# Layer-1 experts that write their results straight to the output, in a two-layer graph network on one core

## The reference

```
# x: (3125, 256), after layer 1's two attentions were added to it
xf = layernorm(x)                                  # the normed rows
idx = argmax(xf @ router_w.T + router_b, axis=-1)  # one of 32 experts per row
h   = relu(xf @ W1[idx] + b1[idx])                 # 256 -> 64
y   = relu(h @ W2[idx] + b2[idx])                  # 64 -> 256
out = x + y                                        # x is the row before the norm
```

## Time and profile before

| | kernel before |
|---|---|
| median of three runs | 3251.31 us |
| the profiled execution, its own time | 3242.09 us |
| its span (first to last instruction) | 3240.5 us |
| instructions | 49670 |
| PE / DVE / POOL / ACT busy, of the span | 69% / 64% / 53% / 38% |
| mean granted TensorE clock | 0.795 of full speed |

### The profile page before, as it was taken

The page is one execution under the profiler, slowest core; times in us unless marked ns, Lnnn a source line. Parts: engine busy times, 40 slices in busy tenths (PEclk is TensorE's granted clock), DMA queues, the critical chain, the costliest instruction groups (busy, mean ns, idle before and its releaser), DMA issues. The chain is left out here.

```text
span 3240.5 us, 49670 instructions
## 1 busy us (share of the span) xinstructions
PE 2249.1 (69%) x10992; PEld 1511.7 (47%) x10993; DVE 2061.8 (64%) x3849; ACT 1246.3 (38%) x3616; POOL 1712.3 (53%) x1802
## 2 busy tenths in 40 slices
PE   3635887867997389948674799997662666654693
PEld 2322333345555356525563678776552444433341
DVE  7587777778888343352576788887593656665221
ACT  3223333326775212233101567765201667652010
POOL 1586777733554301132554877774466777751213
PEclk9866777678999599979776899998755989885555
DMA  4768888875785278835996788886896555530444
GB/s 140 206 181 234 262 260 261 264 231 144 218 217 157 101 252 284 265 94 185 370 395 207 236 270 281 278 280 167 248 312 175 150 147 147 148 103 23 132 152 132
DMA packets 456711, 673.21 MB, mean 208 GB/s; under 512 B 67154, under 2 KB 333836, under 8 KB 456001
## 3 DMA queue, kind: packets, MB, share of 16 engines
q1 hardware_dynamic: 334017, 357.96, 35.9%
q0 software_dynamic: 87248, 263.43, 27.2%
q10 hardware_dynamic: 35296, 50.06, 4.3%
HBM read 494.85 MB, written 177.80 MB: 208 GB/s over the span
## 5 line engine op out<-in xcount | busy, mean ns | idle before, releaser
L1532 POOL DMA_INDIRECT xn<-table,src_col x572 | 591.1, 1033 | 180.0 <-issue 156.2
L1573 PE MATMUL sum_h_ps<-xn,sum_h_hot 128*128 128x261 f32 (+1 forms) x1936 | 530.6, 417 | 185.8 <-DVE xn L1587 142.7
L1573 PEld LDWEIGHTS sum_h_ps<-xn,sum_h_hot 128*128 128x128 f32 x1936 | 371.7, 202 | 336.8 <-DVE xn L1587 241.7
L1092 POOL DMA_INDIRECT arena_a<-table,src_col x264 | 265.2, 1005 | 270.2 <-issue 184.6
L978 POOL DMA_INDIRECT arena_b<-table,src_col x336 | 318.5, 948 | 111.7 <-issue 109.6
L1587 DVE TENSOR_TENSOR xn<-xn,al 128x514 f32<-128x514 f32 (+1 forms) x352 | 243.5, 692 | 161.8 <-DMA xn<-table,src_col 158.5
L1596 DVE TENSOR_TENSOR arena_a<-arena_a,sum_h_ps 128x522 f32 (+1 forms) x440 | 246.1, 559 | 64.8 <-issue 41.1
L1706 PE MATMUL sum_ps<-xn,sum_hot 128*128 128x264 f32 x880 | 245.8, 407 | 31.1 <-DVE arena_a L1729 10.9
L999 PE MATMUL score_ps_hd<-arena_a,score_hot 128*128 x1320 | 254.7, 346 | 0.0
L1689 POOL TENSOR_TENSOR xn<-xn,al 128x264 f32<-128x264 f32 x220 | 154.9, 706 | 171.8 <-DMA xn<-edge_h 169.8
L1009 ACT ACTIVATE xn<-score_ps_en 128x512 f32<-128x512 f32 x220 | 131.5, 598 | 293.3 <-PE score_ps_en L995 289.1
(11 more groups left out here) (516 smaller groups left out, 4632.9 us busy)
## 6 DMA issues: line engine op xcount, KB each, us to landing
xn<-edge_h SPq DMA_DIRECT2D x220, 264.0 KB, 3.1
edge_h<-arena_b SPq DMA_DIRECT2D x84, 528.0 KB, 4.6
arena_b<-kept SPq DMA_DIRECT2D x66, 516.0 KB, 5.3
xn_t<-edge_rows SPq DMA_DIRECT2D x110, 256.0 KB, 4.6
score_h_hot<-hots SPq DMA_DIRECT2D x220, 128.0 KB, 13.4
kept<-arena_a ACTq DMA_DIRECT2D x40, 516.0 KB
xn<-kept SPq DMA_DIRECT2D x66, 257.0 KB
arena_a<-in_f_w SPq DMA_DIRECT2D x16, 1024.0 KB, 8.5
```

The source lines that it names most:

```text
L1092: pool.indirect_dma_start(rows[:, q, s, :], None, table, bass.IndirectOffsetOnAxis(ap=K.src_col[:, w * SUB + s:w * SUB + s + 1], axis=0)). ...
L1532: pool.indirect_dma_start(rows[w][:, s, 0:RW], None, table, bass.IndirectOffsetOnAxis(ap=K.src_col[:, w * SUB + s:w * SUB + s + 1], axis=0 ...
L1573: ins = pe.matmul(ps[:, u, b, 0:part], lhsT=hot[:, w % QH, s, :], rhs=rows[w][:, s, b * part:(b + 1) * part], start=(s == 0), stop=(s == S ...
```

## The change

- `slots1` rows become 513 words (2052 bytes) wide: the normed row, the row before the norm (the token sum `x`), and the node's number as an integer. `finish_route_l1` builds these rows in `arena_a`: DVE's second addition writes to `total_x` there and not to `K.x`, ACT's norm writes beside it, and POOL writes the numbers with one `iota`. Since `arena_a` also holds what the additions read, the chunks go from the last tiles to the first (`tile_of`).
- The earlier blanking writes zeros and the number 3125 in each row, in 28 DMAs for the 14 of before, each of about the same size.
- In `experts_l1` the load brings 2052-byte rows. DVE's `result` first copies the numbers to a small tile, then computes relu(PSUM) + x in one instruction (`scalar_tensor_tensor`). POOL scatters the result by the numbers into the output; rows with number 3125 are out of bounds and left out. Since `result` now reads the rows' buffer, the next load into it waits for the result (`s_yb`) and not for `down` (`s_y`). The weights' load keeps its wait on `s_y`.
- `combine_l1` is gone, and with it the array `y_slots1`.

```diff
@@ segment_softmax
-        blanks = K.slots1.shape[0] // (4 * P) if H == H0 else 0
-        zeros = K.arena_b[:, 5 * 1024:6 * 1024]
+        blanks = K.slots1.shape[0] // (2 * P) if H == H0 else 0
+        zeros = K.arena_b[:, 5 * 1024:5 * 1024 + 2 * SLOT1]
...
-                    sp.dma_start(K.slots1[r * 4 * P:(r + 1) * 4 * P, :].rearrange("(p j) d -> p (j d)", j=4), zeros[:, :]).then_inc(s_blank, 16)
+                    sp.dma_start(K.slots1[r * 2 * P:(r + 1) * 2 * P, :].rearrange("(p j) d -> p (j d)", j=2), zeros[:, :]).then_inc(s_blank, 16)
...
-                pool.memset(zeros[:, :], 0.0).then_inc(s_zeros, 1)
+                pool.memset(zeros[:, :], 0.0).then_inc(s_wiped, 1)
+                pool.wait_ge(s_wiped, 1)
+                pool.iota(zeros.rearrange("p (j d) -> p j d", j=2)[:, :, 2 * D].bitcast(I32), [[0, 2]], base=NOBODY, channel_multiplier=0).then_inc(s_zeros, 1)
@@ finish_route_l1
+        both = K.arena_a[:, :].rearrange("p (t r) -> p t r", t=NT)
+        xn, total_x, token = both[:, :, 0:D], both[:, :, D:2 * D], both[:, :, 2 * D].bitcast(I32)
+        def tile_of(n):
+            return NT - U - n // U * U + n % U
...
+            pool.wait_ge(s_gone, 1)
+            pool.iota(token, [[P, NT]], base=FIRST_TOKEN, channel_multiplier=1).then_inc(s_token, 1)
+            pool.wait_ge(s_token, 1)
             pool.wait_ge(s_slot, 1)
             for t in range(NT):
-                pool.indirect_dma_start(K.slots1, bass.IndirectOffsetOnAxis(ap=K.slot_to[:, t:t + 1], axis=0), K.xn[:, t, :], None).then_inc(s_sent, 16)
+                pool.indirect_dma_start(K.slots1, bass.IndirectOffsetOnAxis(ap=K.slot_to[:, t:t + 1], axis=0), both[:, t, 0:SLOT1], None).then_inc(s_sent, 16)
...
+                if c == chunks - 1:
+                    dve.sem_inc(s_gone, 1)
...
-                    ins = dve.scalar_tensor_tensor(K.x[:, t, :], K.tab2[:, t, 0:D], f2[:, t, 0:1], K.x[:, t, :], ALU.mult, ALU.add)
+                    ins = dve.scalar_tensor_tensor(total_x[:, t, :], K.tab2[:, t, 0:D], f2[:, t, 0:1], K.x[:, t, :], ALU.mult, ALU.add)
@@ experts_l1
-        sizes = {"rows": D, "w": 2 * F1 + D, "xs_t": 2 * P, "h_t": P, "y": D}
+        sizes = {"rows": SLOT1, "w": 2 * F1 + D, "xs_t": 2 * P, "h_t": P, "y": D}
+        token = st.sbuf("token", [P, Q], I32)
...
-                pe.wait_ge(s_yb, j + 1)
+                pe.wait_ge(s_yb, j + 1 + Q - U2)
...
-                act.wait_ge(s_y, j + 1)
+                act.wait_ge(s_yb, j + 1)
                 act.dma_start(rows[:, q, :], K.slots1[bass.ds(j * P, P), :]).then_inc(s_in[q], 16)
...
-                dve.tensor_scalar(y[:, q, :], ps_y[:, q % U2, 0:D], 0.0, None, ALU.max).then_inc(s_yb, 1)
+                dve.tensor_copy(token[:, q:q + 1], rows[:, q, 2 * D:SLOT1].bitcast(I32))
+                dve.scalar_tensor_tensor(y[:, q, :], ps_y[:, q % U2, 0:D], 0.0, rows[:, q, D:2 * D], ALU.max, ALU.add).then_inc(s_yb, 1)
...
-            dve.sem_inc(s_yb, U2)
+            dve.sem_inc(s_yb, Q)
...
-                    pool.wait_ge(s_yb, j + 1 + U2)
+                    pool.wait_ge(s_yb, j + 1 + Q)
                     pool.nop(nofuse=True)
-                    pool.dma_start(K.y_slots1[bass.ds(j * P, P), :], y[:, q, :]).then_inc(s_out[q], 16)
+                    pool.indirect_dma_start(out, bass.IndirectOffsetOnAxis(ap=token[:, q:q + 1], axis=0), y[:, q, :], None,
+                                            bounds_check=N - 1, oob_is_err=False).then_inc(s_out[q], 16)
@@ combine_l1: removed whole
```

More of the change, by code:

```diff
@@ L165, in norm_tiles, with chunk_moments @@
     return T
-def chunk_moments(dve, step, K, T, c, s_var):
+def chunk_moments(dve, step, x, T, c, s_var):
     part = slice(c * U, (c + 1) * U)
@@ L423, in _ @@
             for c in range(NT // U):
-                chunk_moments(dve, step, K, T, c, s_var)
+                chunk_moments(dve, step, lambda t: K.x[:, t, :], T, c, s_var)
             for c in range(NT // U):
@@ L2566, in _ @@
             pe.wait_ge(s_w, 32)
-            for t in range(NT):
-                pe.wait_ge(s_xn, t + 1)
-                if t >= 2:
-                    pe.wait_ge(s_xt, t - 1)
-                pe.transpose(ps_x[:, t % 2, 0:P], K.xn[:, t, 0:P], K.ident[:, :])
-                pe.transpose(ps_x[:, t % 2, P:D], K.xn[:, t, P:D], K.ident[:, :]).then_inc(s_turn, 1)
-                if t >= 1:
-                    logits_of(t - 1)
+            for n in range(NT):
+                t = tile_of(n)
+                pe.wait_ge(s_xn, n + 1)
+                if n >= 2:
+                    pe.wait_ge(s_xt, n - 1)
+                pe.transpose(ps_x[:, n % 2, 0:P], xn[:, t, 0:P], K.ident[:, :])
+                pe.transpose(ps_x[:, n % 2, P:D], xn[:, t, P:D], K.ident[:, :]).then_inc(s_turn, 1)
+                if n >= 1:
+                    logits_of(n - 1)
             logits_of(NT - 1).then_inc(s_logits, 1)
@@ L2589, in _ @@
             for c in range(chunks):
-                chunk_norm(act, K, T, c, s_var, s_std, s_rstd, s_xn)
-                for t in range(c * U, (c + 1) * U):
-                    act.wait_ge(s_turn, t + 1)
-                    act.activation(K.xn_t[:, :, t * P:(t + 1) * P], ps_x[:, t % 2, 0:D].rearrange("p (k n) -> p k n", k=2), ACT.Copy).then_inc(s_xt, 1)
+                part = slice(c * U, (c + 1) * U)
+                act.wait_ge(s_var, c + 1)
+                act.activation(T["std"][:, part], T["var"][:, part], ACT.Sqrt, bias=K.eps[:, 0:1]).then_inc(s_std, 1)
+                act.wait_ge(s_rstd, c + 1)
+                for n in range(c * U, (c + 1) * U):
+                    act.activation(xn[:, tile_of(n), :], total_x[:, tile_of(n), :], ACT.Identity, scale=T["rstd"][:, n:n + 1], bias=T["shift"][:, n:n + 1]).then_inc(s_xn, 1)
+                for n in range(c * U, (c + 1) * U):
+                    t = tile_of(n)
+                    act.wait_ge(s_turn, n + 1)
+                    act.activation(K.xn_t[:, :, t * P:(t + 1) * P], ps_x[:, n % 2, 0:D].rearrange("p (k n) -> p k n", k=2), ACT.Copy).then_inc(s_xt, 1)
         @block.vector
@@ L2794, in _ @@
                     j = i * Q + q
-                    pool.wait_ge(s_yb, j + 1 + U2)
+                    pool.wait_ge(s_yb, j + 1 + Q)
                     pool.nop(nofuse=True)
-                    pool.dma_start(K.y_slots1[bass.ds(j * P, P), :], y[:, q, :]).then_inc(s_out[q], 16)
+                    pool.indirect_dma_start(out, bass.IndirectOffsetOnAxis(ap=token[:, q:q + 1], axis=0), y[:, q, :], None,
+                                            bounds_check=N - 1, oob_is_err=False).then_inc(s_out[q], 16)
             for q in range(Q):
                 pool.wait_ge(s_out[q], 16 * turns)
-def combine_l1(prog, K, out):
-    with Stage(prog, "join1") as st:
-        y = K.xn
-        s_y = [st.sem_sw(f"y{c}") for c in range(NT // U)]
-        s_sum, s_out = st.sem("sum"), st.sem("out")
-        block = st.block()
-        @block.gpsimd
-        def _(pool):
-            st.clear_stale(pool)
-            for t in range(NT):
-                pool.indirect_dma_start(y[:, t, :], None, K.y_slots1, bass.IndirectOffsetOnAxis(ap=K.slot_to[:, t:t + 1], axis=0)).then_inc(s_y[t // U], 16)
-        @block.vector
-        def _(dve):
-            for c in range(NT // U):
-                dve.wait_ge(s_y[c], 16 * U)
-                part = y[:, c * U:(c + 1) * U, :]
-                dve.tensor_tensor(part, part, K.x[:, c * U:(c + 1) * U, :], ALU.add).then_inc(s_sum, 1)
-        @block.sync
-        def _(sp):
-            for c in range(NT // U):
-                sp.wait_ge(s_sum, c + 1)
-                whole = U if c < NT // U - 1 else U - 1
-                sp.dma_start(out[c * U * P:(c * U + whole) * P, :].rearrange("(t p) d -> p t d", p=P), y[:, c * U:c * U + whole, :]).then_inc(s_out, 16)
-            sp.dma_start(out[(NT - 1) * P:N, :], y[0:NLAST, NT - 1, :]).then_inc(s_out, 16)
-            sp.wait_ge(s_out, 16 * (NT // U + 1))
 def stages(prog, K, A, out):
@@ L2853, in stages @@
     finish_route_l1(prog, K, A)
-    experts_l1(prog, K, A)
-    combine_l1(prog, K, out)
+    experts_l1(prog, K, A, out)
 class Keep:
```

24 lines of the change are left out of this document (13 added, 11 removed).

## The result

The changed kernel takes 3329.78 us (median of 4 runs, 3323.89 to 3331.93), the kernel before 3254.18 us on the same chip (4 runs, 3249.6 to 3258.67). The ratio is 1.0237, with a 95% interval of 1.0222 to 1.0252: slower by some 76 us, where 28 us less had been forecast. The profiled execution took 3331.93 us, its span is 3330.4 us.

What follows compares the result with a forecast made beforehand. A circle of waits through load latency, not PE, was taken to pace the experts' loop. Terms -43.0 + 14.3 + 0 + 0.3 + 0.4 = -28.0 us took 3251.3 to 3223.3 us; range 3210 to 3244, 8 times in 10.

Steps and rivals of the forecast that it cites:

- rival 3: Layer 0's blanking outgrows its stage: at 204 GB/s it ends some 18 us past it; 3241 us, chance 0.04.
- Blanking: Layer 0's zero writes: 14.7 MB for 7.3, taking 36 to 40 us, hidden behind DVE; cost 0.
- Only the last landing counts: Layer 1 routing: 25 scatters cost POOL what they did; only the last one lands later, +0.4 us (0 to +0.8).
- The sentence on the Trainium skill: Rows' load in the experts' loop: descriptors off 256-byte boundaries fetch unused bytes; under 2 us in all.
- The end of the program: Adding stage removed, last scatter and a 4.6 us DRAIN now at the end; -43.0 us.
- The order of the link: Experts' loop: load, PE's transposes, `down`, next load, 6.00 us; waiting for `result` makes the last part 1.95 for 1.40.
- The loop: Experts' loop: the load's wait for `result` adds 0.55 us a link over 26 links, +14.3 us.
- step (b): Experts' loop: rows' load of 257 KB for 128, taken as 0; bounds -4.2 to +12.0 us in all.
- rival 1: Experts' loop: the load's size counts in full, +0.46 us a link, +12.0 us; 3235.3 us, chance 0.22.
- Rival 2: Experts' loop: loads land as with busy DMA engines, 5.3 us for 3.0, +60; 3283 us, chance 0.06.
- rival 4: Experts' loop: scatters don't hide or another circle closes, +26 to +43 us; 3235 to 3252, chance 0.06.
- The start of the loop: Experts' loop: three loads of twice the size ahead of the first weights, +0.3 us (0 to +1).

Runs made afterwards that it cites:

- wait_result: Kernel before with one wait moved: the load waits for DVE's result, not for the second matmul; 3238.06 us for 3242.7, ratio 0.9983.
- p520: Changed kernel with slots1 rows 520 words (2080 bytes) long and apart; 3218.05 us for 3239.66 of the kernel before, ratio 0.9934.
- joined: Write-only stage added to a kernel with 2080-byte rows: 12 DMAs of 4104-byte pieces side by side; 42.7 us.
- odd: Same added stage: 12 DMAs of 2052-byte pieces, two a partition, side by side; 42.5 us.
- near_odd: Added write-only stage: 25 POOL scatters of 128 rows of 2052 bytes, each DMA's rows side by side; median landing 15.3 us.
- woven: Added write-only stage: 4104-byte pieces side by side, but neighbouring pieces given to successive DMAs; 36.5 us for 12 DMAs.
- even: Added write-only stage: 12 DMAs of 4096-byte pieces side by side; 16.9 us.
- quad: Added write-only stage: 12 DMAs of 4112-byte pieces side by side; 18.7 us.
- apart: Added write-only stage: 12 DMAs of 4104-byte pieces placed every 4160 bytes, with a gap; 17.0 us.
- both shifts: Added write-only stage: two groups of 12 DMAs, 4096-byte pieces every 4160 bytes, starting 8 or 4 bytes in; 17.0 and 17.7 us.
- far: Added write-only stage: 12 DMAs of 2052-byte pieces, two a partition, every 2112 bytes, starting 4 bytes in; 19.6 us.
- far_odd: Added write-only stage: 25 POOL scatters of 2052-byte rows, a row's neighbours in the DMAs before and after; landing 2.8 us.
- near_pair: Added write-only stage: 25 POOL scatters of 128 rows of 2056 bytes, each DMA's rows side by side; 3.7 us for 3.0.
- pair: Added write-only stage: 12 DMAs of 2056-byte pieces, two a partition, side by side; 22.3 us.
- the skips: Added write-only stage: two groups of 12 DMAs, 4104-byte pieces every 8208 bytes, starting at 0 or 4104; 23.1 and 22.3 us.
- probe_sent: Kernel with 2080-byte rows and eight loop buffers, plus a write-only stage of three SP groups and four POOL scatter groups; 3449.84 us, before 3244.68.

## Why the prediction was wrong

The time lies 86 us above the range's upper end of 3244. The sign was decided by writes that the prediction had set at 0.0 and 0.4 us. Its rival 3 names the first of the places, with a chance of 0.04 and a price of 18 us where 74 were lost.

**The steps that failed.**
- *"Blanking: ... 36 us, to 741, or 40 us at 370. Cost 0; the cover is gone below ... 272 GB/s."* The cover was sized well, the rate was not: 114 GB/s in place of 407 to 370, 129 us in place of 36 to 40, +74.2 us. The row taken as the nearest was that of 2064-byte rows, 16 bytes times 129; the new pieces were 4104 bytes side by side. Nearness was judged by size, and what decided, as far as the runs tell, was where the pieces meet. Rival 3 came close ("pieces of 4104 bytes at odd addresses": it is not the address alone, a start off by 8 bytes cost 0.1 us in 17) but halved the rate by choice, to 204 GB/s, without a row that bounds it. No row of before bounds it well. In one stretch rows of 1028 bytes, an odd number of words as here, are stored side by side, and the DMA engines stand at 0.79 and move 212 GB/s; the queues' rows of the same stretch (packets, MB, share) show whose time that is:

```profile
2440.00:2460.00 20.00, 2.45 (x12) 1.80 (x10) 1.58 (x4) 0.00 (x0) 15.13 (x17) 0.64 0.79 212
```
```profile
q0 software_dynamic: 767, 2.10, 48.3%
q10 hardware_dynamic: 2204, 2.13, 30.9%
```

The stores (q10) move 2.13 MB at a share of 0.309, that is 345 GB/s at a full share; it is the gathers of 1028-byte rows (q0) that stand at 217. They stand at 269 (a share of 0.378 for 6.11 MB) from 2560 to 2620, where no such store runs, so the stores may cost them something. It is a warning at most, not a rate.

- *"257 KB in 1.29 us is 204 GB/s, half of what the engines do. Only the last landing counts: +0.4 us."* True at 2080 bytes (206 GB/s at a share of 0.53, routing 112.4 us), wrong at 2052: the engines do 80 to 156 GB/s, a backlog forms behind an issue that looks unchanged, and +29.3 us stand at the stage's end. The test that I gave for it (more than 1.3 us a scatter on POOL) couldn't find this: POOL only issues. What tells is the landing and the distance from the last issue to the DRAIN.
- The sentence on the Trainium skill stands beside this. The Trainium skill, page "DMA: Bandwidth & Descriptors", section "How a descriptor splits into AXI transactions", was weighed as the rule against such rows. It speaks of reads, and no run here sets rows of this length on and off such a boundary for reading; for writes the trace gives it next to nothing: a start off by 8 bytes, with a gap, took 17.0 us for 16.9. Another page of the Trainium skill, "Collectives: The Full Stack", section "Rules for kernel authors", asks for 32-byte aligned buffers, to prevent a read-modify-write in the hardware; it speaks of collectives, and I had not weighed it. It points in the direction of the loss, but 32 bytes is not what these runs show: rows of 2064 bytes, whose every second boundary is off 32, lost nothing.

**The terms that held.** The end of the program: behind the last scatter's landing a DRAIN of 4.62 us (forecast 4.6), and 9.8 us from the start of tile 54's result to the end for the 9.5 rebuilt, so -42.7 us for -43.0. The order of the link, and 1.96 us from `down` to the next issue for the 1.95 worked out. The scatter in the loop hidden (970 ns, landing in 2.4 us, POOL waiting for DVE). POOL's cost of the routing scatters, 0.97 and 0.30 us.

**The terms that were mis-sized.** The loop: +14.3 forecast. From the load of tile 7 to that of tile 55 are 24 links and 154.2 us (3158.57 to 3312.8), for 145.3 before: +0.37 us a link, 8.9 us for the 13.2 that 0.55 a link makes over them. The cause is step (b), the cost of the load, taken at 0: it has two parts with opposite signs. Going half a microsecond behind the weights gives 0.70 us back (wait_result), and the longer row, with the scatter, takes 0.48 (changed kernel against wait_result). The first was seen in the prediction and valued at 0.16; the second is near rival 1's 0.46. Net 2.80 for 3.02. Rival 2 (landings of over 4 us in the circle) and rival 4 (a scatter or another circle that paces the loop) have nothing in the rows for them. The start of the loop cost +1.2 us (20.9 from the first load to tile 7's, 19.7 before) for 0.3.

**What the change does without the slow writes.** In p520 the same table gives 0 for the softmax-and-sums stage, -0.2 for the routing, +11.3 for the experts, -43.5 for the end and +3.7 for the edges' scores: -28.7 us; timed, -21.6 us, with an interval of -28 to -15. The forecast of -28 was thus near the worth of the change as meant, at the edge of what was timed, and partly by luck: +3.7 us that I had not seen stand against 4 too many in the experts' stage.

**What stays open.** Which unit it is that neighbours share. A shared block of 16 bytes explains joined, odd, near_odd and woven on one side and even, quad, apart, both shifts, far and far_odd on the other. It doesn't explain why 2056-byte rows, of which every second boundary is off 16, lose so little (near_pair 3.7 us for 3.0; pair 22.3 us against odd's 42.5), nor the 22 to 23 us of the skips, nor why the 1028-byte rows that the kernel before stores side by side show no loss in their own share. That a read and a write back of the shared block is behind it was only argued, from the rates; no run shows the reads. Whether gathers of odd rows cost more in themselves (269 GB/s at a full share for 1028-byte rows; for 2064-byte rows, from 1560 to 1600, 4.94 MB at 0.316, that is 391) has no run of its own. And the 3.5 us of the edges' scores.

## What to carry to other kernels

When a row that is written to DRAM gets a word more, look at where it ends, not only at how long it is: pad the pitch to a multiple of 16 bytes (three words here; one word did nearly as well) before anything else is judged, for rows scattered side by side as for blanket writes. A DMA share near 1 isn't a rate; read the GB/s beside it, and for POOL's indirect DMAs the landing, since the issue looks the same when the engines fall behind. A circle of load, compute and buffer release is better cut by more buffers than paid for: eight for four took 20 us from the experts' stage of the kernel before and 29 us from that of p520.

## What the runs showed of the hardware

- Writes to DRAM whose pieces share a boundary off 16 bytes with a piece in flight at the same time: 42.7 us for 6.3 MB in place of 16.9 (148 for 372 GB/s), and 114 GB/s over 14.7 MB in the kernel. With a gap, or with the neighbours issued 1.27 us apart, nothing of it (17.0 us; landing 2.8 us for 15.3).
- Loads of such rows lose nothing by the pitch in the experts' loop: the stage is 192.9 us long with a pitch of 2052 bytes and 193.9 with 2080, the landing 2.7 us in both.
- Two loads issued together on two queues, 128 KB of rows and 192 KB of weights: 3.02 us from the rows' issue to PE's start, and 2.32 us when the rows' load goes half a microsecond later (means over 45 links), a gain larger than the delay.
- Where POOL has itself waited for its DMAs' landings, the closing DRAIN of its queue is 2.09 us after 25 of them, 4.62 after 56, stores before and scatters now, and 8.2 after the 100 scatters of probe_sent.
